# A vision tower with a mixture of experts on one core: the shared expert in one piece, the last expert combined by one-hot matmuls, weights by chunk

## The reference, cut to what matters

```python
probs = softmax(xt @ router_w + router_b)
rw, ids = top_k(probs, 2)
rw = rw / (sum(rw) + 1e-20)
for e in range(8):
    w_e = sum(where(ids == e, rw, 0.0))
    y = y + w_e * _ffn(xt, gate_w[e], up_w[e], down_w[e])   # silu(x@g) * (x@u) @ d
y = y + _ffn(xt, sh_gate_w, sh_up_w, sh_down_w)
h = h + y
h1 = layernorm(h)            # (x - m) / sqrt(v + 1e-5)
n1 = rmsnorm(h1, norm1_w)    # x * rsqrt(mean(x * x) + 1e-6) * w
```

## Time and profile before

| | |
|---|---|
| median of three runs | 428.79 us |
| the profiled execution | 428.56 us, its span 426.6 us |
| TensorE busy | 364.1 us (85%), granted clock 0.90 in the mean |
| VectorE, ScalarE, POOL busy | 250.6, 179.5, 139.0 us |
| DMA | 37.31 MB, mean 87 GB/s |
| first attention and embedding | 0 to about 112 us |
| shared chunks, router, scatter | about 119 to 160 us |
| eight experts | about 160 to 279 us |
| up to the first matmul of the next layer | to 315.7 us |

### The profile page before, as it was taken

The page is one execution under the profiler, slowest core; times in us unless marked ns, Lnnn a source line. Parts: engine busy times, 40 slices in busy tenths (PEclk is TensorE's granted clock), DMA queues, the critical chain, the costliest instruction groups (busy, mean ns, idle before and its releaser), DMA issues.

```text
span 426.6 us, 7295 instructions
## 1 busy us (share of the span) xinstructions
PE 364.1 (85%) x2956; PEld 299.9 (70%) x2956; DVE 250.6 (59%) x619; ACT 179.5 (42%) x372; POOL 139.0 (33%) x76
## 2 busy tenths in 40 slices
PE   4997477998979948889888988988469999899997
PEld 3764246886758948889888988974126788578865
DVE  1568973999765613444434344437654687666874
ACT  2010633223024414666666666331016884286900
...
GB/s 295 402 158 2 0 0 65 140 13 2 0 2 0 137 172 215 139 173 218 149 162 160 186 134 88 51 58 61 250 0 0 2 2 0 0 2 2 2 0 57
DMA packets 15995, 37.31 MB, mean 87 GB/s; under 512 B 1914, under 2 KB 9841, under 8 KB 15960
## 3 DMA queue, kind: packets, MB, share of 16 engines
...
## 4 chain that ended last, share of the span: by engine, by line
PE 51%; DVE 23%; issue 16%; POOL 4%; DMA 3%; ACT 2%; SPq 0%; POOLq 0%; DVEq 0%
PE ps L1416 10%; PE ps L1417 8%; PE ps L1418 8%; DVE stage_l L774 2%; PE ps L1600 2%; PE ps L1702 2%; PE ps L1341 2%; PE ps L1669 2%; PE ps L1245 2%; DMA stage_l<-in_tokW 2%; DVE xn L724 2%; DVE stats L678 2%; PE ps L1353 1%; POOL rstd L1138 1%; PE ps L1610 1%
## 5 line engine op out<-in xcount | busy, mean ns | idle before, releaser
L1138 POOL TENSOR_TENSOR rstd<-vtmp,cst 128x5 f32<-128x5 f32 x6 | 7.1, 1182 | 168.1 <-DVE vtmp L709 115.8
L952 DVE TENSOR_TENSOR ps<-gact,ps 128x256 f32<-128x256 f32 (+3 forms) x60 | 26.2, 437 | 50.8 <-ACT gact L492 44.5
L1202 POOL TENSOR_TENSOR w1l<-raw,w1h 128x1536 fp32r<-128x1536 f32 (+1 forms) x12 | 39.6, 3305 | 32.2 <-ACT w1h L507 32.1
L1202 POOL TENSOR_TENSOR w0l<-raw,w0h 128x1536 fp32r<-128x1536 f32 (+1 forms) x12 | 39.8, 3313 | 25.4 <-ACT w0h L507 25.4
L492 ACT ACTIVATE gact<-ps 128x256 f32<-128x256 f32 (+3 forms) x60 | 23.3, 389 | 33.9 <-PE ps L1418 27.4
L957 DVE TENSOR_TENSOR hrl<-ps,hrh 128x256 fp32r<-128x256 f32 (+1 forms) x48 | 20.4, 425 | 21.6 <-ACT hrh L496 21.6
L1238 PE MATMUL ps<-cst 128*128 128x512 f32 x66 | 32.4, 641 | 0.0
L1416 PE MATMUL ps<-xg0h,w1h 128*128 128x256 f32 x88 | 25.8, 294 | 5.6 <-issue 4.1
L1416 PE MATMUL ps<-xg1h,w0h 128*128 128x256 f32 x88 | 25.8, 293 | 5.5 <-issue 5.5
L496 ACT ACTIVATE hrh<-ps 128x256 fp32r<-128x256 f32 (+1 forms) x48 | 18.4, 384 | 26.1 <-DVE ps L952 25.1
L1417 PE MATMUL ps<-xg1l,w0h 128*128 128x256 f32 x88 | 24.9, 283 | 0.0
...
## 6 DMA issues: line engine op xcount, KB each, us to landing
raw<-in_wexp SPq DMA_DIRECT2D x18, 768.0 KB, 4.4
...
xg_d<-zero SPq DMA_DIRECT2D x8, 256.0 KB, 10.8
xgs<-xg_d SPq DMA_DIRECT2D x8, 256.0 KB, 5.3
yg_d<-y SPq DMA_DIRECT2D x8, 256.0 KB, 3.9
...
```

The source lines that it names most:

```text
L952: V.tensor_tensor(up, gact[i % 2][rows_of(c), 0:n], up, ALU.mult).then_inc(S("hm"), 1)
L1202: nc.gpsimd.tensor_tensor(wset[x % 2][1][w], raw[w], wset[x % 2][0][w].bitcast(F32), ALU.subtract).then_inc(S("w_lo"), 1)
```

## The change

The shared expert is computed whole before the experts (`NH` is 12 units), and `tw` is gone. Weights are laid out by chunk: part 0 now holds gate and up of chunks 0 to 2, part 1 those of chunks 3 to 5. ScalarE makes the pieces of the next weights two chunks earlier, those of weights 1 ahead of the norm. `xgs` has two buffers, filled one expert at a time. The last expert's result is not stored and gathered: the slot numbers of expert 7 are compared with `iota` to a one-hot matrix, which TensorE turns (`turn_one_hot`) and multiplies with the result (`last_rows`). Adds of shared and gathered rows move into experts 5 and 7, router weights into expert 0. `vo` and `km` have memory of their own and are cleared at the start of the kernel. The weights of the last layers are loaded behind the last store, before the branch. The two powers behind the experts are one, over 10 columns: 1/sqrt(v + 1e-5), and 1/sqrt(v/(v + 1e-5) + 1e-6); `xn` is made from `h` with their product, `xres` later.

The diff, cut to its core (left out: declarations, the branch, and `rest`, which restricts sources and weights to experts 0 to 6):

```diff
-WPART = (DC * GP, DC * GP + DC * P, FC * D)
-WOFF = (0, DC * GP, 2 * DC * GP + DC * P)
-WMIX = 2 * DC * GP
+CHW = 2 * DC * P
+WMIX = CHW * (FC - 1)
+WPART = (3 * CHW, 2 * CHW + DC * P, FC * D)
+WOFF = (0, WPART[0], WPART[0] + WPART[1])
...
-CH = 4
-NH = 2 * CH
-NE = NH + FC * E
-TG, TM, TD = 0, 2 * DC * P, 3 * DC * P
-TW = TD + (FC - CH) * D
+NH = SU
...
-        xgs = eb("xgs", [P, E, CT, D], F32)
+        xgs = [eb(f"xgs{i}", [P, CT, D], F32) for i in range(2)]
...
+        turned = hs[0]
+        onehot = yrow[0][:, 0:3, :].rearrange("p a d -> p (a d)").bitcast(BF16)[:, 0:TT * CAP].rearrange(
+            "p (t s) -> p t s", t=TT)
+        iota_s = yrow[0][:, 3, 0:CAP]
+        ylast = [x[:, 0:CT, :] for x in hr]
...
             next_load(2, 0)
+            next_load(2, 1)
+            def load_rows(e):
+                if e >= 2:
+                    sp.wait_ge(S("xt_mm"), e - 1)
+                sp.dma_start(xgs[e % 2][:, :, :], xg_d[e * T:e * T + CAP].rearrange(
+                    "(s p) d -> p s d", p=P)).then_inc(S(f"d_xg{e % 2}"), 16)
+
             sp.wait_ge(S("d_sent"), 32 * TT)
-            for e in range(E):
-                sp.dma_start(xgs[:, e], xg_d[e * T:e * T + CAP].rearrange("(s p) d -> p s d", p=P)).then_inc(
-                    S(f"d_xg{e}"), 16)
-            next_load(2, 1)
+            load_rows(0)
+            load_rows(1)
+            sp.wait_ge(S("expert_done"), 1)
+            sp.dma_start(iota_s, iota).then_inc(S("d_iota"), 16)
             next_load(2, 2)
-            for x in range(3, E + 1):
-                for part in range(3):
-                    next_load(x, part)
-                store_y(x - 3)
+            next_load(3, 0)
+            for e in range(E - 2):
+                next_load(e + 3, 1)
+                next_load(e + 3, 2)
+                if e + 4 <= E:
+                    next_load(e + 4, 0)
+                load_rows(e + 2)
+                store_y(e)
...
-            store_y(E - 1)
+            for dst, src in ((kvd_s, kvd), (wl1["g"]["wq"], wqg), (wl1["g"]["wo"], wog),
+                             (wl1["l"]["wq"], wql), (wvl_s, wvl), (wl1["l"]["wo"], wol),
+                             (wfin_s, wfin)):
+                sp.dma_start(dst[:], src).then_inc(S("d_l1"), 16)
+            sp.dma_start(kug_s[:, :], kug).then_inc(S("d_l1"), 16)
+            sp.dma_start(vug_s[:, :], vug).then_inc(S("d_l1"), 16)
...
-            sp.wait_ge(S("moe"), 1)
-            for dst, src in ((kvd_s, kvd), (wl1["g"]["wq"], wqg), (wl1["g"]["wo"], wog),
-                             (wl1["l"]["wq"], wql), (wvl_s, wvl), (wl1["l"]["wo"], wol),
-                             (wfin_s, wfin)):
-                sp.dma_start(dst[:], src).then_inc(S("d_l1"), 16)
-            sp.dma_start(kug_s[:, :], kug).then_inc(S("d_l1"), 16)
-            sp.dma_start(vug_s[:, :], vug).then_inc(S("d_l1"), 16)
...
+            def weights_hi(x, piece):
+
+                part, n = piece // 2, WPART[piece // 2] // 2
+                o = WOFF[part] + piece % 2 * n
+                act.wait_ge(S(f"d_raw{part}"), 16 * x + 16)
+                if x == 2 and part < 2:
+                    act.wait_ge(S("gu"), (6, NH)[part])
+                if x > 2 and part < 2:
+                    act.wait_ge(S("gu"), NH + FC * (x - 3) + (3, FC)[part])
+                if x >= 2 and part == 2:
+                    act.wait_ge(S("expert_done"), x - 1)
+                A(wset[x % 2][0][:, o:o + n], raw[:, o:o + n], ACT.Copy).then_inc(S("w_hi"), 1)
+
+            for piece in range(6):
+                weights_hi(1, piece)
...
-            for cols in HALVES:
-                A(xTh[:, :, cols], xnT[:, :, cols], ACT.Copy).then_inc(S("xTh"), 1)
+            for k in range(DC):
+                A(xTh[:, k, :], xnT[:, k, :], ACT.Copy).then_inc(S("xTh"), 1)
...
             for u in range(NH):
                 shared(u, u // 2, u % 2)
-                if u < 6:
-                    weights_hi(1, u)
+                if u >= NH - 2:
+                    weights_hi(2, u - (NH - 2))
...
-                    if e + 2 <= E:
-                        weights_hi(e + 2, c)
+                    if c < 4 and e + 2 <= E:
+                        weights_hi(e + 2, c + 2)
+                    if c >= 4 and e + 3 <= E:
+                        weights_hi(e + 3, c - 4)
                     if c == 3 and e + 1 < E:
                         gathered_hi(e + 1)
...
-            for v in range(SU - NH):
-                shared(NE + v, CH + v // 2, v % 2)
+            act.wait_ge(S("expert_done"), E + 1)
+            A(ylast[0].rearrange("p s d -> p (s d)"), bank(7), ACT.Copy).then_inc(S("y7h"), 1)
...
-            for hf, cols in enumerate(HALVES):
-                dve.wait_ge(S("xTh"), hf + 1)
-                V.tensor_tensor(xTl[:, :, cols], xnT[:, :, cols], xTh[:, :, cols].bitcast(F32),
+            for k in range(DC):
+                dve.wait_ge(S("xTh"), k + 1)
+                V.tensor_tensor(xTl[:, k, :], bank(4 + 2 * k, 2)[:, 0:TP], xTh[:, k, :].bitcast(F32),
                                 ALU.subtract).then_inc(S("xTl"), 1)
...
+            def one_hot(t):
+                dve.wait_ge(S("d_iota"), 16)
+                V.tensor_scalar(onehot[:, t, :], iota_s, slot[:, t, E - 1:E], None,
+                                ALU.is_equal).then_inc(S("onehot"), 1)
+
+            def take_turned(s):
+                dve.wait_ge(S("oh_mm"), s + 1)
+                V.tensor_copy(turned[:, s, :], psb[:, 6 * BK:6 * BK + TP]).then_inc(S("turned"), 1)
+
+            def add_shared(t):
+                dve.wait_ge(S("expert_done"), 1)
+                V.tensor_tensor(h[:, t, :], h[:, t, :], bank(t // 2)[:, (t % 2) * D:(t % 2 + 1) * D],
+                                ALU.add).then_inc(S("h_acc"), 1)
+
+            def add_rows(which, w, t):
+                m = slice(0, min(P, T - t * P))
+                dve.wait_ge(S("h_acc"), TT + which * (t + 1))
+                if which == 0:
+                    dve.wait_ge(S("d_lo"), 16 * TT)
+                else:
+                    dve.wait_ge(S(f"d_hi{t}"), 16)
+                V.scalar_tensor_tensor(h[m, t, :], yrow[which][m, t, :], w[m, t:t + 1], h[m, t, :],
+                                       ALU.mult, ALU.add).then_inc(S("h_acc"), 1)
+
+            def add_last(t):
+                dve.wait_ge(S("h_acc"), 2 * TT + t + 1)
+                dve.wait_ge(S("last_mm"), t + 1)
+                V.scalar_tensor_tensor(h[:, t, :], bank(LAST[t])[:, 0:D], wts[:, t, E - 1:E], h[:, t, :],
+                                       ALU.mult, ALU.add).then_inc(S("h_acc"), 1)
...
-                steps = {0: destinations, 2: router_probs, 3: overflow, 4: sources, 5: weights_of_each}
-                if u in steps:
-                    steps[u]()
+                if u == 1:
+                    destinations()
...
+            steps = {0: router_probs, 1: overflow, 2: sources, 4: weights_of_each}
...
+                    if e == 0 and c in steps:
+                        steps[c]()
...
+                    if e == 2 and c < TT:
+                        one_hot(c)
+                    if e in (3, 4) and c == FC - 1:
+                        take_turned(e - 3)
+                    if e == 5 and c < TT:
+                        add_shared(c)
+                    if e == E - 1 and c >= 3:
+                        for step in (((0, 0), (0, 1), (0, 2)), ((0, 3), (0, 4), (1, 0)), ((1, 1), (1, 2)))[c - 3]:
+                            add_rows(step[0], (wlo, whi)[step[0]], step[1])
+            dve.wait_ge(S("y7h"), 1)
+            V.tensor_tensor(ylast[1].rearrange("p s d -> p (s d)"), bank(7),
+                            ylast[0].rearrange("p s d -> p (s d)").bitcast(F32), ALU.subtract).then_inc(S("y7l"), 1)
+            add_rows(1, whi, 3)
+            add_rows(1, whi, 4)
+            norm_count[0] += TT
             for t in range(TT):
-                dve.wait_ge(S("y_all"), 1)
-                link(V.tensor_tensor(h[:, t, :], h[:, t, :], bank(t // 2)[:, (t % 2) * D:(t % 2 + 1) * D],
-                                     ALU.add))
-            dve.wait_ge(S("d_hi"), 16 * TT)
-            add_rows(1, whi)
-            V.memset(zero[:, 0:1], 0.0).then_inc(S("y_read"), 1)
-
-
-            dve.wait_ge(S("y_read"), 1)
+                add_last(t)
+                dve.wait_ge(S("h_acc"), 3 * TT + t + 1)
+                tile_stats(h, t)
+
...
+                    aggregate()
+                    link(V.tensor_scalar(pair[:, 0, :], mv[:, :, 1], LN_EPS, None, ALU.add))
+                    link(V.reciprocal(pair[:, 1, :], pair[:, 0, :]))
+                    link(V.tensor_tensor(pair[:, 1, :], pair[:, 1, :], mv[:, :, 1], ALU.mult))
+                    V.tensor_scalar(pair[:, 1, :], pair[:, 1, :], RMS_EPS, None, ALU.add).then_inc(S("var"), 1)
+                    root()
+                    link(V.tensor_tensor(both_roots[:, :], roots[:, 0, :], roots[:, 1, :], ALU.mult))
+                    for t in range(TT):
```

(82 more changed lines are left out.)

232 lines of the change are left out of this document (82 added, 150 removed).

## The result

The changed kernel takes 443.52 us (median of four runs, 442.56 to 443.72) against 429.13 for the kernel before: a ratio of 1.037, 95% interval 1.031 to 1.043. The prediction was 433.5 with a range of 414 to 446 and 0.57 for slower. The range holds the time and the sign is right; the size is three times the forecast, and the time lies above the 426 to 440 that the prediction gave its own case. Some executions of a kernel are a few per cent longer than its others, and times here are medians over all while ratios leave the long ones out, which matters for e2_rows_first (422.6 us over the six shorter of ten executions, 425.24 over all) and for e5, e10 and e11, on whose chip the kernel before has 424.8 us over the five shorter of twelve and 429.7 over all.

What follows compares the result with a forecast made beforehand. TensorE, half of the chain, was taken as the bound through its waits and clock; terms of +1.0, -10.4, +19, +10.5, +3, +1.8, +1.5, -20.4, -1.3 sum to +4.7: 428.56 + 4.7 + 0.2 = 433.5 us, range 414 to 446.

Steps and rivals of the forecast that it cites:

- its own case: Whole kernel: the prediction's main case, 433.5 us, range 426 to 440, chance 0.52.
- The new wait: Expert loop, turns 2 to 6: TensorE waits for rows behind weight loads, 5 by 3.8 us, +19.
- The clock: Expert loop: TensorE's clock falls to half after each of five new waits, 5 by 2.1 us, +10.5.
- Rival 1: Expert loop: the clock holds through the new waits, 423 us; chance 0.18.
- rival 2: Expert loop: the rows land in time, so wait and clock terms go, 406 us; chance 0.15.
- VectorE's steps: Experts 0 and 2: router steps and one-hot compares on VectorE, mostly hidden by slack, +3 us, ends 0 and 13.
- rival 3: Expert 2: five compares wait out POOL's subtractions, +12, 443 us; chance 0.15, shared with ScalarE's whole stall.
- The removed wait: Expert starts: TensorE's wait for w_lo goes, seven boundaries by 1.5 us, -10.4.
- Tail: Last gate matmul to the next layer's first matmul: 39.4 us becomes 19.0, -20.4, ends 17 and 22.
- Front: Up to turn(0): added shared-expert matmuls mostly fill a TensorE hole, +1.0 us, ends -1 and +5.
- ScalarE's stall: Front: ScalarE's 6.4 us idle before shared unit 6; -1 without it, +5 with the whole again.
- next layer: Start of the next layer: less work at half clock, -1.3 us, ends 0 and -2.7.

Runs made afterwards that it cites:

- e2_rows_first: Changed kernel with the gathered rows issued at the same late moment but ahead of the 768 KB weight load on SP: 425.24 us, ratio 0.991.
- e5: Changed kernel with the last layers' nine weight loads held back until the five lower gathers have landed: 441.25 us, ratio 1.043.
- e10: Kernel of e9_all with POOL's clears of vo and km begun behind identb: 411.00 us, ratio 0.970 to the kernel before.
- e11: Kernel of e9_all unchanged, run again on the chip of e10: 412.52 us, ratio 0.972 to the kernel before.
- e9_all: Changed kernel with rows loaded early, compares on POOL, router steps in shared units, gathered-row adds out of expert 7: 409.09 us, ratio 0.946.
- e8_before_pieces: Kernel before, with ScalarE making each piece of the next weights one chunk earlier: 423.33 us, ratio 0.976.
- e12: Kernel of e9_all with seven instead of nine clock-keeping matmuls before the next layer's transposes: 412.78 us, ratio 0.962 to the kernel before.

## Why the prediction was right, and where it was off

**The new wait.** Right in place, cause and size: five waits, 16.9 us against 19, behind the load on SP's queue. The one at turn 3 is 2.24, because TensorE came late to it itself.

**The clock.** Right: five falls, 10.7 us against 10.5. Rival 1 (the clock holds) and rival 2 (the rows are in time) did not come about.

**VectorE's steps, the step that failed most.** The prediction gave them 3 us, with ends of 0 and 13, on the argument that VectorE has over 1 us of slack in a chunk. In the loop TensorE waited 9.7 us for VectorE or for what stands behind it (the list above without its first and fifth rows; the fifth, 1.4, was there before). Moving the compares and the router steps away measured 3.1 and 4.3 us, 7.4 together; with both away, in e9_all, 3.3 us of such waits are left, mostly for `take_y`, which the next term is about. The slack is real, but an operation of 0.2 to 0.34 us that meets a subtraction takes 1.3 to 2.8, which is more than the slack. That is rival 3's mechanism at a quarter of its price, 3.1 us for 12: three of five compares met POOL, not five. What the rival left out are the router steps, which cost more. The Trainium skill (SBUF — State Buffer, section Who interferes with whom) says the same of a VectorE instruction with two SBUF inputs beside a GpSimd instruction that reads SBUF, and the trace agrees (1.53 and 1.28 us for such steps of 35 to 40 elements).

**The removed wait.** Predicted -10.4. In e8_before_pieces it measures 7.4, since `take_y` is next in line. In the changed kernel this second wait is part of the 9.7.

**Tail.** Predicted -20.4, measured -16.2. The term that was mis-sized is the chain of the last products: 2.9 us forecast, 7.5 in the trace (309.45 to 316.97), through two adds that wait for gathers. The prediction had the gathers late at one place (1.3 us, behind the last products) and charged the adds in expert 7 with 1.5 us; it did not ask what a wait of such an add holds up on its own engine. The transposes behind the nine clock-keeping matmuls add 0.8. The power over 10 columns cost 0.8 more than over 5 (1.99 against 1.17), with 1.0 forecast; `wfs` held nothing back.

**Front.** +2.9 against +1.0. The shared stage itself took 42.5 us, as before (42.7), because ScalarE's stall did not come in this execution; that is the prediction's end without a stall (-1), measured at -0.2. The +3.1 lies ahead of it, at the first loads, where the prediction had no term. Of the eleven experiments with the changed front, e5 had no stall either and took 42.5 us. Seven had it and took 44.8 to 48.2. The three others, e10 to e12, had no stall, but a router step that met POOL's subtraction (3.9 us) and took 47.8 to 49.1. The median of the eleven is 46.0, 3.3 more than before, so the end of +5 was nearer to the usual case than the +1.0.

Sum of the differences: front +1.9, loop +4.8, tail +4.2, next layer -0.5, in all 10.4 us: the 15.1 measured on the spans less the 4.7 forecast. The loop's +4.8 is mainly the waits for VectorE (9.7 for the 3 of its steps, +6.7) and the half clock at its start (+1.9), less 2.1 of waits for the rows and the 1.5 for the adds in expert 7, which showed in the tail.

That the range held the time is in part luck. Its upper end, 440 to 446, stood for rival 3 or ScalarE's whole stall; neither came as described, and the time got there by a loop, a tail and a front that were each priced 2 to 5 us too low.
